# A state-space and attention block on one core: the next batch's front moved into the directions

## What is computed

```python
xz = einsum('bchw,oc->bohw', gn(x), in_proj_w)          # 96 -> 2 x 192 channels
xx, z = split(xz, 2)
u = gelu(depthwise_conv3x3(xx, conv_w) + conv_b)         # the front
xs = [u, u^T, reversed u, reversed u^T]                  # K = 4 directions
dts, B, C = split(einsum(xs, x_proj_w), [12, 28])        # 12, 16 and 16 rows
delta = softplus(einsum(dts, dt_w) + dt_b)
for t in range(L):                                       # 192 channels x 16 states
    h = h * exp(delta[t] * A) + delta[t] * u[t] * B[t]
    y[t] = sum_n(h * C[t]) + u[t] * D
out = x + out_proj(layernorm(sum of 4 directions) * gelu(z))
```

## Time and profile before

| | us |
|---|---|
| three runs | 11191.21 median, 11173.36 to 11194.83 |
| profiled execution | 11183.75, span 11181.9 |
| PE busy | 7561.9 (68%) |
| DVE busy | 8288.1 (74%) |
| ACT busy | 6339.2 (57%) |
| POOL busy | 6348.7 (57%) |
| mean granted TensorE clock | 0.783 |
| HBM traffic | 1186 MB read, 215 MB written |

### The profile page before, as it was taken

One profiled execution on the slowest core, in us unless ns is written; L12 is line 12 of the kernel. 1 busy time (PEld: TensorE's weight loads), 2 busy tenths in 40 slices (PEclk: granted clock), 3 DMA queues, 4 the chain that ended last, 5 costly groups with the idle time before them and its releaser, 6 DMA issues.

```text
span 11181.9 us, 192632 instructions
## 1 busy us (share of the span) xinstructions
PE 7561.9 (68%) x53104; PEld 2446.8 (22%) x53104; DVE 8288.1 (74%) x11547; ACT 6339.2 (57%) x11827; POOL 6348.7 (57%) x4028
## 2 busy tenths in 40 slices
PE   4665478873788638885488845887458873788758
PEld 1221122221222212221122211222112221222212
DVE  4998668865889658896599955998669876689630
ACT  3332357743677437773377734776357753677468
POOL 3785447744677337764278633875347744577320
PEclk7555579975899759996599956998579985899779
DMA  3554145531555225551355513555135541455310
GB/s 90 179 178 147 24 143 180 176 106 32 165 184 172 77 56 172 184 165 53 81 176 186 160 35 102 177 181 155 30 116 177 183 129 25 147 182 175 101 23 19
DMA packets 686795, 1410.24 MB, mean 126 GB/s; under 512 B 74400, under 2 KB 334272, under 8 KB 678080
## 3 DMA queue, kind: packets, MB, share of 16 engines
q1 hardware_dynamic: 686016, 1401.21, 41.2%
HBM read 1186.22 MB, written 214.70 MB: 125 GB/s over the span
## 4 chain that ended last, share of the span: by engine, by line
issue 49%; POOL 18%; PE 14%; DVE 8%; DMA 5%; ACT 4%; SPq 1%; POOLq 1%; DVEq 0%; ACTq 0%
POOL hc_buf L692 9%; PE ps L1369 3%; PE ps L1399 2%; PE ps L1400 2%; DMA rep<-bc_scratch 2%; PE ps L1222 2%; DVE ps L996 2%; DVE job_buf L1020 1%; POOL job_buf L309 1%; DVE rings L1020 1%; POOL job_buf L330 1%; ACT probs_buf L796 1%; POOL job_buf L337 1%; DMA hc_buf<-y_scratch 1%; PE ps L1441 1%
## 5 line engine op out<-in xcount | busy, mean ns | idle before, releaser
L796 ACT ACTIVATE probs_buf<-ps 128x384 f32<-128x384 f32 x6912 | 3071.2, 497 | 1738.8 <-PE ps L1288 1719.8
L692 POOL TENSOR_TENSOR hc_buf<-rings,rep 128x768 f32<-128x768 f32 x1152 | 2095.0, 1819 | 2257.1 <-DVE rings L1020 2253.0
L996 DVE TENSOR_TENSOR ps<-ps,rep 128x384 f32<-128x384 f32 x4608 | 2534.6, 551 | 620.9 <-PE ps L1197 420.4
L1197 PE MATMUL ps<-st_buf,pick_channel 96*128 96x384 bf16 x4608 | 1676.4, 364 | 1217.1 <-DVE rings L1020 713.6
L692 POOL TENSOR_TENSOR hc_buf<-job_buf,rep 128x768 f32<-128x768 f32 x1152 | 2094.3, 1818 | 523.3 <-DVE job_buf L1020 509.4
L1288 PE MATMUL ps<-qp_buf,kp_buf 108*128 108x384 bf16 (+1 forms) x6912 | 2172.2, 344 | 115.7 <-ACT job_buf L766 47.5
L1222 PE MATMUL ps<-probs_buf,v_buf 128*13 128x384 f32 x13824 | 1541.0, 520 | 31.8 <-ACT probs_buf L796 17.9
L1210 PE MATMUL ps<-hc_buf,sum_states 128*32 128x144 f32 x24576 | 1451.3, 322 | 111.8 <-POOL hc_buf L692 111.8
L787 ACT ACTIVATE st_buf<-st_buf,a_cols 128x768 f32<-128x768 f32 x1152 | 1080.6, 938 | 283.9 <-DMA st_buf<-delta_scratch 280.5
L787 ACT ACTIVATE rings<-rings,a_cols 128x768 f32<-128x768 f32 x1152 | 1078.2, 937 | 185.6 <-DMA rings<-delta_scratch 185.6
L1288 PEld LDWEIGHTS ps<-qp_buf,kp_buf 108*128 108x128 bf16 x6912 | 659.8, 98 | 2113.3 <-ACT probs_buf L796 973.7
(11 more groups left out here) (161 smaller groups left out, 9530.7 us busy)
## 6 DMA issues: line engine op xcount, KB each, us to landing
st_buf<-delta_scratch SPq DMA_DIRECT2D x1152, 384.0 KB
rings<-delta_scratch SPq DMA_DIRECT2D x1152, 384.0 KB
part_scratch<-job_buf SPq DMA_DIRECT2D x1152, 72.0 KB, 2.1
st_buf<-part_scratch SPq DMA_DIRECT2D x192, 432.0 KB, 7.0
rep<-bc_scratch SPq DMA_DIRECT2D x192, 384.0 KB
delta_scratch<-job_buf SPq DMA_DIRECT2D x192, 192.0 KB, 4.8
qp_buf<-qk_scratch SPq DMA_DIRECT2D x864, 36.0 KB
kp_buf<-qk_scratch SPq DMA_DIRECT2D x432, 72.0 KB
```

The costliest lines, as they stand in the source:

```text
L692: pool.tensor_tensor(hc[tile % 2][:, chunk(kk, v)], h_ring[t % 2], rep_third(1, kk, v), ALU.mult).then_inc(s["hc_ready"], 1)
L796: act.activation(probs[(m % 2) * HG + h], bank(slots["score", p]), ACT.Exp, scale=SCALE)\
L996: dve.tensor_tensor(bu, bu, rep_piece(0, kk, v), ALU.mult)\
L1197: pe.matmul(bank(BANK_U[x % 3]), pick(x // 2), st[x // 2 // SPG][:, piece(v)], start=True, stop=True)\
```

## The change

The work of `front` is cut into steps of the directions (`front_step(fb, f, t)`: stretch f, step t) of the batch before. Stretch 0 normalises x in place and stores it. Stretches 1 to 6 handle a chunk of 8 image rows each: load ten rows, project, nine taps as matmuls with diagonal weights for 128 channels, nine for 64, GELU, x_proj, and store u and the projections to HBM. Stretches 7 and 8 make the projections of the transposed u. All of it uses one PSUM bank, which is taken from the score ring. Direction 3 makes the next batch's first jobs. Jobs now load their operands from HBM, and the back loads u. For batch 0 the same steps stand one after another in `start`. The loop over stretches is written out. SBUF for the new buffers comes from `u_buf`, `dts` and smaller rings.

```diff
-SCAN_RING = 3
+SCAN_RING = 2
+FRONT = K * NS - NS
-JOB_START = (1, 7, 13)
+LOAD_JOB = (0, 4, 10)
+JOB_START = (3, 8, 14)
-        u_buf = sb("u_buf", [128, 2 * L])
-        dts = sb("dts", [128, L])
+        conv_w = [sb("conv_w_a", [128, 9 * 128]), sb("conv_w_b", [64, 9 * 64])]
+        BANK_F, BANK_U, BANK_Y, BANK_PV = 2, (3, 4, 5), 6, 7
 def batches(...):
-            front(0); directions(0, None); back(0)
-            with engine.Fori(1, NB) as b:
-                front(b); directions(b, b - 1); back(b)
+            start(); enter(0); directions(0, None, True); back(0)
+            with engine.Fori(1, NB - 1) as b:
+                enter(b); directions(b, b - 1, True); back(b)
+            enter(NB - 1); directions(NB - 1, NB - 2, False); back(NB - 1)
 def stretches(engine, body):
-            body(0, True)
-            with engine.Fori(1, NS) as q:
-                body(q, False)
+            for q in range(NS):
+                with engine.Fori(0, 1):
+                    body(q, q == 0)
 # SP
+            def enter(b):
+                    sp.wait_ge(s["n_mul"], b * NORMS)
+                    store_parts(b - 1)
+                    first_queries_keys()
+                    sp.wait_ge(s["v_ev"], b * 5)
+                for i in range(SPT):
+                    load_rep(b, 0, i)
+                for n in range(LEAD):
+                    first_deltas(b * K, 0, n)
...
+                for g in range(2):
+                    load_st(0, g)
+            def load_job(b, kidx, k, q, j):      # at steps 0, 4, 10
...
+                    sp.dma_start(job_d[:, piece(j)], d_src[r:r + R, cols]).then_inc(job_loaded[j], 16)
+                    sp.dma_start(job_u[:, piece(j)], u_src[0:DA, cols]).then_inc(job_loaded[j], 16)
 def back(b):                                     # SP
+                    sp.dma_start(u[1][p, :], of_batch(u_dram, b)[0, 0, DA:DI, hf * HL:(hf + 1) * HL])\
+                      .then_inc(s["y_loaded"], 16)
+                sp.dma_start(u[0], of_batch(u_dram, b)[0, 0, 0:DA, :]).then_inc(s["y_loaded"], 16)
 # PE
+            def front_step(fb, f, t):
+                elif f <= CHUNKS:
+                    if t == 4:
+                        pe.wait_ge(s["f_chunk"], (n + 1) * 16)
+                        pe.matmul(bank(BANK_F, n=XC), in_proj[:, 0:DA], xc[:, :], start=True, stop=True)
+                    if t == 6:
+                        pe.wait_ge(s["f_pad"], 2 * n + 1)
+                        pe.matmul(bank(BANK_F, 64, XC), in_proj[:, DA:DI], xc[:, :], start=True, stop=True)
+                    if 8 <= t < 13:
+                        conv_taps(0, 2 * (t - 8))
+                    if 14 <= t < 19:
+                        conv_taps(1, 2 * (t - 14))
+                    if t == 21:
+                        pe.wait_ge(s["f_gelu"], 2 * n + 2)
+                        # two products with x_proj
+                else:
+                    # at steps 5, 11, 17: two products with x_proj on the transposed u
+            def conv_taps(i, tap0):
+                for tap in range(tap0, min(tap0 + 2, 9)):
+                    ins = pe.matmul(square(bank(BANK_F, p)), conv_w[i][:, tap * p:(tap + 1) * p],
+                                    window(pads[i][:, :], tap, 8), start=(tap == 0), stop=(tap == 8))
 # ACT
+            def front_step(fb, f, t):            # t 5, 7: copy 480 columns to the pads; t 13: copy
+                    if t == 19:
+                        act.activation(uc[1][:, :], bank(BANK_F, 64), ACT.Gelu, bias=conv_bias[1][0:64, :])
+                        act.activation(uc[0][:, :], uc[0][:, :], ACT.Gelu, bias=conv_bias[0][:, :])
+                        act.preload_act_table_set(LN_EXP_TABLES)
+                    if t == 22:
+                        project_out(fb, c)
 # DVE: stretch 0, steps 3 to 10: six bn_stats, bn_aggr, three small operations
 # POOL: stretch 0, steps 13 to 15: normalisation; stretches 2 to 7, steps 1, 2: transposed copies of u
```

More of the change, by code:

```diff
@@ L262, in pad_rows, with at_least, of_batch, chunk_rows @@
             return pad.rearrange("p (h w) -> p h w", w=PADW)[:, r:r + n, 1:1 + W]
-        def front_units():
-            tmp = [rep[:, i * HL:(i + 1) * HL] for i in range(3)]
-            work = [(window(pads[1], tap, H // 2), taps[1][:, tap:tap + 1], square(u[1])) for tap in range(9)]
-            return work, [square(x) for x in tmp], 1, 0, 0
+        def at_least(engine, name, value):
+            if not (isinstance(value, int) and value <= 0):
+                engine.wait_ge(s[name], value)
+        def of_batch(dram, b):
+            return dram[bass.ds(b, 1)]
+        def chunk_rows(c):
+            return (1 if c == 0 else 0), (9 if c == NPC - 1 else 10)
         def back_units():
@@ L728, in back @@
                 apart(pool)
-            batches(pool, front, directions, back, attention)
+            batches(pool, start, lambda b: None, directions, back, attention)
         @block.scalar
@@ L870, in directions @@
+            def directions(b, ab, more):
+                act.preload_act_table_set(LN_EXP_TABLES)
                 for kk in range(K):
[L871 removed]
+                    stretches(act, lambda q, first: stretch(b, kk, q, first, ab, more))
                 if ab is not None:
@@ L937, in attention @@
                 for kk in range(K):
-                    stretches(act, lambda q, first: stretch(None, kk, q, first, ab, False))
+                    stretches(act, lambda q, first: stretch(None, kk, q, first, ab, False, False))
                 last_leftover(ab)
-            batches(act, front, directions, back, attention)
+            batches(act, start, lambda b: None, directions, back, attention)
         @block.vector
@@ L1168, in attention @@
                 for kk in range(K):
-                    stretches(dve, lambda q, first: stretch(None, kk, q, first, ab, False))
+                    stretches(dve, lambda q, first: stretch(None, kk, q, first, ab, False, False))
                 leftover((ab + 1) * STRETCHES, COPY_O)
-            batches(dve, front, directions, back, attention)
+            batches(dve, start, lambda b: None, directions, back, attention)
         @block.tensor
@@ L1467, in attention @@
                 for kk in range(K):
-                    stretches(pe, lambda q, first: stretch(None, kk, q, first, ab, False))
+                    stretches(pe, lambda q, first: stretch(None, kk, q, first, ab, False, False))
                 last_leftover(ab)
-            batches(pe, front, directions, back, attention)
+            batches(pe, start, lambda b: None, directions, back, attention)
 def kernel(**inputs):
```

627 lines of the change are left out of this document (407 added, 220 removed).

## The result

The changed kernel took 12270.28 us (median of 4 runs, 12267.91 to 12284.53) against 11192.01 for the kernel before (4 runs): ratio 1.097, 95% interval 1.0951 to 1.0989. The forecast was 10854 us, its widest range ended at 11180: wrong in sign, and off by 1416 us. The profiled execution has a span of 12268.7 us, 1086.8 more than before.

A forecast was written before the change was run, and what follows sets the result against it. VectorE was taken to bound each direction, 3.0 us a step. From 11183.75 us, -1043 (front), +160 (first front), +44 (back) and +509 (directions) gave 10854 us; own range 10650 to 11080, with rivals 10540 to 11180.

The forecast's parts named there:

- Term 6: Score ring in the directions: two banks instead of three cost 8 us a batch with attention.
- Term 7: Rest of a batch: statistics 4 us, GpSimd 3, job operands and u's store 10, direction 3 with jobs 0.
- Terms 4, 5: Directions, a batch: TensorE's added products 27 us plus 6 for clock falls; ScalarE's GELUs and table loads 18.
- Term 1: Between batches: the exposed front shrinks from 211 to about 62 us, seven times, -1043 us.
- term 3: Back of each batch: reading u again costs 5.5 us, eight times, +44 us.
- Term 2: Start of the kernel: the first batch's front stays exposed and becomes serial, +160 us once, bounds +90 and +260.
- A: Rival, directions: everything fits beside VectorE, a batch costs 30 us and batch 0 20, total 10553 us; chance 20%.
- B: Rival, score ring in every step with attention: two banks couple PE and ScalarE, 0.3 us a step, 11400 us; chance 13%.
- The test I had set for B: Batch 7, where no front runs: VectorE's waits for PE over 40 us a direction would show B.
- C: Rival, tap steps in directions: taps run at the low clock, 6.8 us a step against 3.0, about 11340 us; chance 8%.

The follow-up runs named there:

- b_jobs3: Experiment 5: the kernel before, three score banks kept, only the jobs moved from steps 1, 7, 13 to 3, 8, 14; 11483.65 us.
- b_ring2_jobs: Experiment 4: the kernel before with two score banks instead of three and the jobs at steps 3, 8, 14; 11732.36 us.
- nofront: The changed kernel with the next batch's front left out of the directions, every batch reading batch 0's front; 11556.26 us.
- b_ring2_last: Experiment 6: the kernel before with two score banks, jobs at 3, 8, 14, each job's product behind its step's third score; 11452.07 us.
- 7: The kernel before with two score banks, each job's product behind the third score, jobs at steps 1, 7, 13; 11263.44 us.
- preload: The changed kernel with operands of jobs 0 and 1 issued at steps 20 and 21 of the stretch before; 12050.12 us.
- nofront_best: The changed kernel with operands issued early, each job's product behind the third score, and the front left out of the directions; 10964.29 us.
- experiment 12: The changed kernel with operands issued early, Relu for the convolution's GELU and no table loads; 11939.83 us.
- experiment 15: The changed kernel with operands early, job products behind the third score, and the taps' weights and padded image in bf16; 11431.52 us.

## Why the prediction was wrong

The stages of the profiled executions (us); a batch's directions go from its first broadcast to the end of GpSimd's last product with C, the gap from there to the next first broadcast:
```
kernel          start  8 x directions  mean gap x 7   end    span
before            214            7104      455 x 7    682   11182
b_jobs3           215            7408      453        683   11478
b_ring2_jobs      213            7654      455        685   11735
nofront           401            8171      327        689   11553
after             407            8859      331        687   12269
```
Down the column of directions stands what the directions lose: +304 for the jobs' places and +246 for the second bank; +517 for the loads of the jobs' operands, the jobs in direction 3 and whatever else of the change is not the front (smaller rings, the loop written out); +688 for the front. Together +1755, where the prediction had +509. The parts overlap (the third bank was worth 246 in the old kernel, 199 without the front, and 158 with the jobs' products last at the old steps, 11263 against 11106), so this is one order of adding them.

**Term 6, two score banks: 56 us predicted, 246 measured; and the jobs' new steps: no term, 304 measured.** This is the step that failed most. I priced the ring from the average distance of scores, and a score behind a score does fit in it (direction 3, no jobs: +6 us). I put 0.7 us a stretch on den, proj and jobs without looking at who frees a job's bank: ScalarE's second read, behind three exponentials. And I did not price the new JOB_START at all: the diff shows the jobs moved by one or two steps, and I named no term for it. Experiments 4 and 5 show both costs, 6 and 7 what order and steps give back, without any other part of the change. Inside the 304 the held bank (experiment 5), the full steps and falls of the clock were not separated.

**Term 7, job operands 48 us and direction 3 at 0: 517 measured with all that stands beside them.** I saw that they queue behind B, C and deltas "at a direction's start". They do so in each stretch, and worst in the second, where `load_rep` stands ahead. By preload 220 us is the queue's. Direction 3 with jobs but no front took 257 us in nofront against 231 without jobs (b_ring2_jobs), 26 us where I had 0, and 171 over all batches. My argument was that direction 3 had been as long without jobs as the others with them. That compared two stages with different starts (in batch 4 of the kernel before, direction 3 has 14.0 us of excess in its first three steps, direction 1 has 10.6), not one stage with and without. With operands early and products last, nofront_best still has 221 us more in its directions than b_ring2_last, 74 of them in direction 3; the other 147 no run separates.

**Terms 4, 5 and the rest of 7, the front on the engines: 405 predicted, 688 measured,** 98 us a batch for 58. The bursts were there, their size was not right. ScalarE's table loads: 18 a batch predicted, some 16 by experiment 12 (110 / 7). The loads had 1.28 us each and no idle before them; the drain that "ScalarE: Activation LUTs" of the Trainium skill gives (section "What ACT_TABLE_LOAD costs") was not seen, as the prediction had said. The taps: 27 + 6 predicted, at least 44 a batch by experiment 15 (8389 to 8083 us of directions, over seven), since even in bf16 they are not free. That leaves up to 38 us a batch, where the prediction had 9, for the projections, x_proj, copies and statistics; no run separates them. Batch 0 lost as much as the others (1012 us against 916 in nofront), where 45 were predicted.

**Term 1, the gap: 1004 us net of the back's loads predicted, 868 measured.** Against the earlier trace rows, keys are issued as said (36.4 us after the signal, 36.5 predicted), but the loads behind them took 42 us, not 25, so the first broadcast came 78.8 us after the signal, not 62:
```profile
6110.00 11.08 SPq L580 DMA_DIRECT2D kp_buf<-qk_scratch  x27
6121.44 4.81 SPq L452 DMA_DIRECT2D rep<-xd_scratch  x6
6126.75 8.46 SPq L433 DMA_DIRECT2D st_buf<-delta_scratch  x3
6135.34 5.24 SPq L433 DMA_DIRECT2D rings<-delta_scratch  x2
6140.94 3.52 SPq L421 DMA_DIRECT2D st_buf<-part_scratch  x2
```
A delta's issue took 2.8 us here, where I had carried over 0.41 from the keys. The issue of all 13 loads, 5.3 us by my count, took 23 (to 6144.5), and the DMA engines moved 137 GB/s from 6125 to 6145, not the 190 of the earlier trace rows. I had also counted only one of the two loads of 432 KB, and not the next image (0.9 MB), whose load was issued at 6146.9 and may share the last 17 us; what each of these cost was not tested. The back (term 3) grew by 9 us (5.5 predicted). **Term 2, the first start: +160 predicted, +193 measured,** inside its bounds. (Its sum took 15 for the loads of B and C that the text puts at 13, and the 365 us it names for the first front should be 374; both are small beside the miss.)

The misses add up: 190 + 304 (bank, places) + 469 + 283 + 136 + 33 = 1415 us, and 10854 + 1415 = 12269. The sum closes because the stages are cut that way; it does not show that each cause has its right share.

**The rivals.** A is out. B had the banks at 0.3 us in every step with attention, 605 us; they cost 246, at the jobs and not in every step. The test I had set for B (over 40 us of waits in a direction of batch 7) came out at 42.6, with 11.7 of it in the one stall behind a load, so it did not tell B from that. C is out as stated, for batches 1 to 6: a tap record of 128 channels took 485 ns in the middle and up to 1009 when cold, only 40 of the 1296 records of both kinds of taps lasted over 700 ns, and directions 0 to 2 were granted 0.80 to 0.86, not under 0.8. In batch 0, which has no scores and was granted 0.53 to 0.57, 133 of the 216 records were over 700 ns. (The prediction says that no row shows a low clock in a busy direction; direction 0 of batch 0 in the earlier trace rows, at 0.57 with VectorE busy for 201.5 of 208 us, is one, though TensorE was busy for only 128.) And the clock did take part elsewhere: 0.92 in direction 1 of batch 4 before is 2 x 0.08 x 225 = 36 us at the low level, 0.86 after is 83 of 297. Around the 12 us stall:
```profile
10905.00:10915.00 10.00, 7.95 (x73) 2.38 (x65) 9.96 (x16) 7.64 (x15) 8.36 (x7) 0.95 0.61 162
10915.00:10920.00 5.00, 4.21 (x20) 0.98 (x20) 2.42 (x5) 0.65 (x2) 1.81 (x1) 0.50 0.80 201
...
10931.00:10936.00 5.00, 3.77 (x12) 0.77 (x12) 1.12 (x2) 1.45 (x4) 0.00 (x0) 0.50 0.52 145
```
PE was at the low level already in the window ahead of the stall, where it had stood for shorter times (1.45 us for the denominators), and again behind it. It came out of the stall with longer instructions: a group of value products took 1.48 us, which takes 0.84 at the high level. How much of the loss is the clock's own, no run here separates.

## What to carry to other kernels

When a change takes a buffer from a ring, ask for each user of the ring who frees it and what stands behind the next user on the in-order engine; an average rate says nothing of the one long holder. An operand that moves from SBUF to HBM can get the latency of what stands ahead of it on its queue: issue it a stage ahead, and look at each place where a large load is issued first. And read every constant of a diff: three shifted step numbers and one bank fewer cost 550 us, where the shorter gaps gave 868, and the one idea that helped the kernel (the job's product behind the third score, 0.7%) came out of pricing them.

## What the runs showed of the hardware that I had not expected

A load of 192 KB on a queue with 1.6 MB issued in the 3.2 us ahead of it, and a delta and queries behind it, was there 13.8 us after its own issue. Issue itself varies on one queue: in the gap between two batches 0.41 us for a load of keys (72 KB) and 2.8 for a replicated delta (384 KB), but 0.58 for such a delta inside a direction. Diagonal float32 taps between the other matmuls of a direction with scores stayed mostly at the high clock (485 ns a record); in batch 0, without scores, most were long. And short waits of PE, 0.65 and 0.87 us within two, preceded a fall to the low level for about 3 us.
